# A graph network kernel: index lists loaded a group to a partition and turned on chip, weight fusion moved into the first pass

## The reference, cut to what matters

```python
# layer 0
msg = relu(x[src] + edge_attr)
agg = segment_sum(msg, dst)
h = 2 * x + agg
f = gelu(bn1(h) @ W1.T + b1) @ W2.T + b2
x = layernorm(x + bn2(h + f))
# layer 1
m = gelu((x[src] + edge_attr) @ W1m + b1m) @ W2m + b2m
agg = segment_sum(m, dst) / max(degree, 1)
u = gelu(agg @ W1u + b1u) @ W2u + b2u
x = layernorm(x + layer_norm(x + u) * gamma + beta)
```

## Time and profile before

| | |
|---|---|
| median of 3 runs | 2294.37 us (2292.27 to 2295.15) |
| the profiled execution's own time | 2303.09 us |
| its span | 2301.3 us |
| PE busy | 1904.6 us (83%) |
| POOL busy | 1674.7 us (73%) |
| DVE busy | 1469.5 us (64%) |
| ACT busy | 1115.6 us (48%) |
| DMA packets | 375187, 567.87 MB; 74454 of them under 512 B |

### The profile page before, as it was taken

How to read it: one execution, slowest core, us unless ns; L and a number is a source line. 1 busy time by engine, 2 the same in 40 slices (tenths; PEclk the granted TensorE clock), 3 DMA queues, 4 the chain that set the end, 5 groups by cost and what they waited for, 6 DMA issues and landing times.

```text
span 2301.3 us, 36392 instructions
## 1 busy us (share of the span) xinstructions
PE 1904.6 (83%) x9184; PEld 1564.5 (68%) x9184; DVE 1469.5 (64%) x3241; ACT 1115.6 (48%) x2268; POOL 1674.7 (73%) x1673
## 2 busy tenths in 40 slices
PE   2887887888887887878856998989989898898896
PEld 1776666666666766666745777877777777777774
DVE  2555555555555555555546677777777777777774
ACT  3444434434444444434325555655565565565662
POOL 4777777777777777777637777777777777777770
PEclk9999999999999999999979999999999999999996
DMA  9999898888999999999856777777777777777771
GB/s 181 317 303 294 283 289 284 294 291 289 291 299 288 297 294 287 289 295 289 254 152 201 218 219 227 226 217 229 224 223 230 221 219 224 216 232 220 220 208 37
DMA packets 375187, 567.87 MB, mean 247 GB/s; under 512 B 74454, under 2 KB 241618, under 8 KB 375122
## 3 DMA queue, kind: packets, MB, share of 16 engines
q1 hardware_dynamic: 280060, 347.71, 47.9%
q0 software_dynamic: 79872, 218.21, 31.9%
q10 hardware_dynamic: 15190, 1.28, 0.7%
HBM read 500.51 MB, written 66.49 MB: 246 GB/s over the span
## 4 chain that ended last, share of the span: by engine, by line
POOL 47%; DMA 17%; issue 16%; PE 13%; DVE 5%; ACT 1%; DVEq 0%; ACTq 0%; POOLq 0%
POOL m_all L413 47%; DMA m_all<-in_x,src_p 8%; DMA m_all<-y_scratch,src_u 7%; PE bank L738 5%; PE bank L763 2%; DMA node<-in_dst 2%; DVE bank L1042 1%; PE bank L654 1%; DVE m_all L1031 1%; ACT m_all L538 1%; PE bank L692 1%; PE bank L710 1%; PE bank L796 1%; PE bank L720 1%; DVE m_lo L1047 1%
## 5 line engine op out<-in xcount | busy, mean ns | idle before, releaser
L413 POOL DMA_INDIRECT m_all<-in_x,src_p x832 | 862.8, 1037 | 278.7 <-issue 239.0
L413 POOL DMA_INDIRECT m_all<-y_scratch,src_u x832 | 810.9, 975 | 292.9 <-issue 231.5
L738 PE MATMUL bank<-m_all,sel 128*128 128x257 f32 x1664 | 460.4, 402 | 184.1 <-ACT m_all L538 182.9
L796 PE MATMUL bank<-w1m_sb,e_all 128*128 128x256 f32 x2080 | 535.1, 397 | 92.5 <-DVE m_lo L1047 87.2
L538 ACT ACTIVATE m_all<-m_all 128x512 f32<-128x512 f32 x416 | 261.6, 632 | 579.2 <-DVE m_all L1031 577.0
L1031 DVE TENSOR_TENSOR m_all<-m_all,e_all 128x512 f32<-128x512 f32 x416 | 286.9, 693 | 357.3 <-DMA m_all<-in_x,src_p 355.7
L738 PEld LDWEIGHTS bank<-m_all,sel 128*128 128x128 f32 x1664 | 306.0, 194 | 304.1 <-ACT m_all L538 241.0
L796 PEld LDWEIGHTS bank<-w1m_sb,e_all 128*128 128x128 f32 x2080 | 382.5, 195 | 162.1 <-DVE m_lo L1047 77.0
L1042 DVE TENSOR_TENSOR bank<-bank,m_all 128x512 f32<-128x512 f32 x416 | 290.5, 698 | 258.7 <-DMA m_all<-y_scratch,src_u 233.3
L563 ACT ACTIVATE m_hi<-bank 128x512 fp32r<-128x512 f32 x416 | 248.8, 598 | 405.4 <-DVE bank L1042 400.9
L763 PE MATMUL bank<-w1m_sb,ez 128*128 128x256 f32 x1248 | 331.1, 389 | 6.5 <-issue 6.3
(11 more groups left out here) (133 smaller groups left out, 1852.0 us busy)
## 6 DMA issues: line engine op xcount, KB each, us to landing
e_all<-in_edge SPq DMA_DIRECT2D x416, 256.0 KB, 5.7
e_all<-in_edgeT SPq DMA_DIRECT2D x208, 256.0 KB, 4.1
ez<-in_edgeT SPq DMA_DIRECT2D x104, 384.0 KB, 6.6
z_scratch<-zc SPq DMA_DIRECT2D x104, 384.0 KB, 5.5
e_all<-z_scratch SPq DMA_DIRECT2D x104, 256.0 KB, 3.6
m_all<-in_x,src_p POOLq DMA_INDIRECT x832, 5.4
e_all<-in_edgeT SPq DMA_DIRECT2D x104, 128.0 KB
e_all<-z_scratch SPq DMA_DIRECT2D x104, 128.0 KB
```

The costliest lines, as they stand in the source:

```text
L413: pool.indirect_dma_start(out=m_sb[n % ROUND][:, t, :], out_offset=None, in_=table, in_offset=bass.IndirectOffsetOnAxis(ap=sources[:, g, 2 ...
L738: return pe.matmul(psum[:, 0:D + 1], selection[:, u, :].bitcast(F32), m_all[:, slot, u % 2, 0:D + 1], start=(u == 0), stop=(u == TILES - 1 ...
L796: last = pe.matmul(z_bank(s)[:, t * D:(t + 1) * D], eT_sb[s % ERING][:, k, t * P:(t + 1) * P], w1m_sb[:, k, :], start=(k == 0), stop=(k == ...
```

## The change

- The lists are loaded once each, with a group on each partition: ends_f[i] is [104, 1024], from two transfers, 103 rows of 4096 bytes and the last group's row, both on ACT's queue, dst first. The window starts win_i are loaded as before.
- DVE casts a list, subtracts from dst each row's own first entry (win_col), takes the extent by partition, and masks the repeated edges of the last group. PE turns the lists by 32 transposes of [104, 128], 8 for each of rel_p, src_p, rel_u, src_u, with a step of 8 columns for the first order; DVE copies them out of PSUM. The four lists are [128, 8, G] now.
- POOL takes the sources of the first two groups from a tile of their own, src_0, and waits for lists_made 2 (rel_p and src_p copied) before the third group.
- On SP's queue w1m and ez move in between the edge loads, the weights of the fusion go before the others, and src_p's loads are gone.
- The weight fusion, the bias row and the spreading of b2u move from the setup into steps 6 and 9 of PE's first round; ACT's copies go to steps 8 and 11 of its round, DVE's to step 13. PE enters the first pass at lists_made 4.
- The spreading of the window starts is left to the general path.

```diff
@@ tiles
-        src_p, src_u = sb("src_p", [P, G, TILES], I32), sb("src_u", [P, G, TILES], I32)
-        rel_p, rel_u = sb("rel_p", [P, G, TILES]), sb("rel_u", [P, G, TILES])
+        src_p, src_u = sb("src_p", [P, TILES, G], I32), sb("src_u", [P, TILES, G], I32)
+        rel_p, rel_u = sb("rel_p", [P, TILES, G]), sb("rel_u", [P, TILES, G])
+        src_0 = sb("src_0", [P, 2, TILES], I32)
...
+        ends_f = [flat[0:G, i * GROUP:(i + 1) * GROUP] for i in range(2)]
@@ SP
-            sp.dma_start(src_p[:, 0:2, :], ends(src, 0, 2)).then_inc(src_first, 16)
+            sp.dma_start(src_0[:], src[0:2 * GROUP].rearrange("(g p u) -> p g u", p=P, u=TILES)).then_inc(src_first, 16)
...
-            sp.dma_start(src_p[:, 2:full, :], ends(src, 2, full)).then_inc(src_rest, 16)
-            sp.dma_start(src_p[:, full, :], last_ends(src)).then_inc(src_rest, 16)
...
-                        sp.wait_ge(lists_made, 2)
+                        sp.wait_ge(lists_turned, 4)
@@ POOL
             for n in range(2 * PAIRS):
-                gather(x, src_p, n)
-            pool.wait_ge(src_rest, 32)
+                gather(x, lambda g, u: src_0[:, g, u:u + 1], n)
+            pool.wait_ge(lists_made, 2)
             for n in range(2 * PAIRS, M):
                 if n >= ROUND:
                     pool.wait_ge(pair_summed, n - ROUND + 1)
-                gather(x, src_p, n)
+                gather(x, lambda g, u: src_p[:, u, g:g + 1], n)
@@ ACT
-            act.dma_start(dst_i[:, full, :], last_ends(dst)).then_inc(dst_in, 16)
-            act.dma_start(dst_i[:, 0:full, :], ends(dst, 0, full)).then_inc(dst_in, 16)
-            for array, tile in ((src, ends_i[0]), (dst, ends_i[1])):
-                act.dma_start(tile[:, 0:blocks * P].rearrange("t (b p) -> t b p", p=P),
-                              array[0:blocks * P * P].rearrange("(b t p) -> t b p", t=P, p=P)).then_inc(lists_in, 16)
...
+            for i, array in enumerate((dst, src)):
+                act.dma_start(ends_i[i][0:full, :], array[0:full * GROUP].rearrange("(g e) -> g e", e=GROUP)
+                              ).then_inc(ends_in[i], 16)
+                act.dma_start(ends_i[i][full:G, :], array[E - GROUP:E].rearrange("(a e) -> a e", a=1)
+                              ).then_inc(ends_in[i], 16)
...
+                if known(i) and i == 0:
+                    if s == 8:
+                        keep_weights()
+                    if s == 11:
+                        keep_bias()
@@ PE
+            def turn_ends(i, by_place, to):
+                rows = ends_f[i].rearrange("g (p u) -> g u p" if by_place else "g (u p) -> g u p", u=TILES)
+                for u in range(TILES):
+                    last = pe.transpose(bank[to + u // 4][:, u % 4 * G:(u % 4 + 1) * G], rows[:, u, :], ident[0:G, 0:G])
+                last.then_inc(lists_turned, 1)
...
+            pe.wait_ge(ends_ready, 1)
+            turn_ends(0, True, 0)
+            pe.wait_ge(extent_ready, 1)
+            pe.matmul(bank[7][:, 0:1], ones[:], extent[:, 2:3], start=True, stop=True).then_inc(counted, 1)
+            pe.wait_ge(ends_ready, 2)
+            turn_ends(1, True, 2)
+            turn_ends(0, False, 4)
+            pe.wait_ge(general_made, 1)
+            turn_ends(1, False, 6)
+            pe.wait_ge(lists_made, 4)
+            pe.wait_ge(w1m_in, 16)
...
+            def fuse_weights():
+                pe.wait_ge(consts_in, 16 * 7)
...
+                if known(i) and i == 0:
+                    if s == 6:
+                        fuse_weights()
+                    if s == 9:
+                        fuse_bias()
@@ DVE
+            dve.wait_ge(ends_in[0], 32)
+            link(dve.tensor_copy(ends_f[0], ends_i[0]))
+            link(dve.tensor_copy(win_col[0:G, :], ends_f[0][:, 0:1]))
+            link(dve.tensor_scalar(ends_f[0], ends_f[0], win_col[0:G, :], None, ALU.subtract))
+            dve.tensor_reduce(extent[0:G, 0:1], ends_f[0], AX_X, ALU.min)
+            link(dve.tensor_reduce(extent[0:G, 1:2], ends_f[0], AX_X, ALU.max))
...
+            dve.wait_ge(ends_in[1], 32)
+            dve.tensor_copy(ends_f[1], ends_i[1]).then_inc(ends_ready, 1)
             dve.wait_ge(counted, 1)
+            dve.tensor_scalar(general[:], bank[7][:, 0:1], 1.0, None, ALU.min).then_inc(general_made, 1)
+            for i, to in enumerate((rel_p, src_p, rel_u, src_u)):
                 dve.wait_ge(lists_turned, i + 1)
+                for half in range(2):
+                    last = dve.tensor_copy(to[:, 4 * half:4 * half + 4, :],
+                                           bank[2 * i + half][:, 0:4 * G].rearrange("p (u g) -> p u g", g=G))
+                last.then_inc(lists_made, 1)
...
-                positions = rel[:, g, :] if known(g) else rel[:, bass.ds(g, 1), :].rearrange("p a u -> p (a u)")
-                select(q % 2, positions.unsqueeze(2)).then_inc(sel_made, 1)
+                select(q % 2, rel[:, :, g:g + 1] if known(g) else rel[:, :, bass.ds(g, 1)]).then_inc(sel_made, 1)
```

More of the change, by code:

```diff
@@ L84, in build @@
     TURN = 512 - (KD + 1) * WIN
-    assert M == ROUND * C and G > full and KH == 2 * KD and G <= 512 and CHUNK % 2 == 0 and N % 2 == 0
+    assert M == ROUND * C and G > full and KH == 2 * KD and G <= P and CHUNK % 2 == 0 and N % 2 == 0
     chunks = [(c * CHUNK, min(CHUNK, N - c * CHUNK)) for c in range(C)]
@@ L467, in _, with keep_weights, keep_bias @@
             is_general = act.value_load(general[0:1, 0:1], min_val=0, max_val=1)
+            def keep_weights():
+                act.wait_ge(w_fused, 1)
+                for k in range(KD):
+                    act.copy(wmu_sb[:, k, :], bank[2 + k][:]).then_inc(w_kept, 1)
+            def keep_bias():
+                act.wait_ge(w_fused, 2)
+                act.copy(bmu_hi[:], bank[2][0:1, :]).then_inc(w_kept, 1)
             def node_a(i, s):
@@ L622, in _ @@
         def _(pe):
-            pe.wait_ge(win_ready, 1)
-            pe.matmul(bank[7][:, 0:G], ones[0:1, :], win_f[:], start=True, stop=True).then_inc(win_spread, 1)
-            pe.wait_ge(extent_ready, 1)
-            pe.matmul(bank[6][:, 0:1], ones[:], extent[:, 2:3], start=True, stop=True).then_inc(counted, 1)
-            pe.wait_ge(consts_made, 5)
-            for i in range(2):
-                pe.wait_ge(lists_float, i + 1)
-                for b in range(TB):
-                    tiles = min(P, T - b * P)
-                    last = pe.transpose(bank[2 + 2 * i + b // 4][:, b % 4 * P:b % 4 * P + tiles],
-                                        ends_f[i][0:tiles, b * P:(b + 1) * P], ident[0:tiles, 0:tiles])
-                last.then_inc(lists_turned, 1)
@@ L635, in _ @@
-            pe.wait_ge(consts_in, 16 * 8)
-            pe.wait_ge(vt_in, 16)
-            pe.wait_ge(general_made, 1)
-            for i in range(KD):
-                for k in range(KD):
-                    pe.matmul(bank[i][:], w2mT_sb[:, k, i * P:(i + 1) * P], w1u_sb[:, k, :],
-                              start=(k == 0), stop=(k == KD - 1))
-            for k in range(KD):
-                last = pe.matmul(bank[6][0:1, :], vec("b2m", k), w1u_sb[:, k, :], start=(k == 0), stop=(k == KD - 1))
@@ new lines, in _, with fuse_bias @@
+            is_general = pe.value_load(general[0:1, 0:1], min_val=0, max_val=1)
+            def fuse_weights():
+                pe.wait_ge(consts_in, 16 * 7)
+                for i in range(KD):
+                    for k in range(KD):
+                        last = pe.matmul(bank[2 + i][:], w2mT_sb[:, k, i * P:(i + 1) * P], w1u_sb[:, k, :],
+                                         start=(k == 0), stop=(k == KD - 1))
+                last.then_inc(w_fused, 1)
+            def fuse_bias():
+                pe.wait_ge(vt_in, 16)
+                pe.wait_ge(w_kept, KD)
+                for k in range(KD):
+                    pe.matmul(bank[2][0:1, :], vec("b2m", k), w1u_sb[:, k, :], start=(k == 0), stop=(k == KD - 1))
+                pe.matmul(bank[3][:, 0:D], ones[0:1, :], b2u_row[:].rearrange("a k p -> a (k p)"), start=True, stop=True
+                          ).then_inc(w_fused, 1)
@@ L859, in _ @@
             with pe.If(is_general > 0):
+                pe.wait_ge(win_ready, 1)
+                pe.matmul(bank[0][:, 0:G], ones[0:1, :], win_f[:], start=True, stop=True).then_inc(win_spread, 1)
+                fuse_weights()
+                fuse_bias()
                 groups(pe, sums_general, 1, C)
@@ L1218, in first_pass @@
                     selection(rel_p, 0, *after)
+                if known(i) and i == 0 and s == 13:
+                    keep_rest()
                 node_a(i, s)
```

121 lines of the change are left out of this document (42 added, 79 removed).

## The result

| | before | changed |
|---|---|---|
| median of 4 runs, us | 2294.24 (2292.27 to 2295.15) | 2308.64 (2305.29 to 2311.77) |
| profiled execution, us | 2303.09 | 2307.26 |
| span of that execution, us | 2301.3 | 2305.5 |

The changed kernel takes 1.0064 times as long (95% interval 1.0046 to 1.0081): 14.4 us slower, where 11 were forecast.

What follows compares the result with a forecast made beforehand. POOL's gathers were taken to set the pace; POOL going on later, +13.4 us, less the ring wait that goes, 2.45, gave +11 us: 2305 us for the median, range 2295 to 2318, with chance 0.62.

Steps and rivals of the forecast that it cites:

- What bounds it: First pass: POOL's nearly back-to-back gathers set the pace, 1.348 us apart; only 16.5 us of gaps wait for the tensor engine.
- One engine for 103 rows: List loads: a transfer counting 103 on the outside goes through one of the 16 DMA engines, as 103 is prime.
- The landing: Setup: the source list lands at 54 us, sharing one engine with SP's packets and the gathers.
- the bound of 60: Source list's landing: 60 us if all of SP's packets come before the lists on the shared engine.
- From the landing to POOL: Setup: cast, 8 transposes, two copies and semaphores take 4.2 us; POOL goes on at 58.4 instead of 44.96, +13.4 us.
- The wait that goes: Start of first pass: POOL's 2.75 us wait for the first ring slot drops to 0.30, -2.45 us.
- The moved fusion, free: Steps 6 and 9 of the first pass: the moved products cost nothing under the tensor engine's lead; uncovered, 8.6 us.
- Strided selection, free: DVE's selections from positions 416 bytes apart: taken as costing nothing; +8 us if their time doubled.
- The clearing of acc near 4 us: Setup on ACT: the 16.02 us copy that clears acc begins at about 4 us, not 37.93; worth nothing by itself.
- Rival A: List loads spread over all engines, so POOL's hole goes: mid -22 us, 2272 us; chance 0.18.
- Rival B: ACT's queue served first on the one engine: landing at 47, +4 us, 2298 us, or sooner and no difference; chance 0.12.
- Rival C: The first pass's start, not POOL, sets its end: +3 us, or -36 with the lists spread; chance 0.08.

Runs made afterwards that it cites:

- the second job: Follow-up runs in which the kernel before took 2297.88 us; it held the cuts at 96 and 94, 96 with fusion in setup, and 103 rows first on SP.
- 96 rows: Changed kernel with each list's 103 rows loaded as two transfers of 96 and 7 rows: 2279.49 us, 0.9923 of the kernel before.
- 96 rows, fusion in setup: Changed kernel with lists cut into 96 and 7 rows and the weight fusion put back into the setup: 2284.43 us, 0.9928 of the kernel before.
- 94 rows: Changed kernel with each list's 103 rows loaded as transfers of 94 and 9 rows: 2290.89 us, 0.9971 of the kernel before.
- 103 rows, first on SP: Changed kernel with both uncut lists moved from ACT's queue to SP's, ahead of the edge rows: 2300.87 us, 1.0014 of the kernel before.
- the first job: Follow-up runs in which the kernel before took 2698.06 us; lists cut at 96 gave 0.9945 of it, at 94 rows 1.0005.
- the three doses: List transfers of 103, 94 and 96 rows in the changed kernel; source list there at 58.14, 36.62 and 15.35 us or sooner.
- the first and third jobs: Follow-up runs in which the kernel before took 2698.06 and 2680.07 us; the third reran the changed kernel (1.007) and the cut at 96 (0.9909).

## Why the prediction was right

The start of gather 33 orders all runs of the comparison and of the second job. Its shift against the kernel before, as a part of 2294 to 2298 us, beside the ratio; the last gather of the pass, number 832, shows whether the pass ends by as much earlier or later:

| kernel | first product, shift | gather 33, us | shift | gather 832, shift | gather 33 as a ratio | measured |
|---|---|---|---|---|---|---|
| 96 rows | -34.4 | 44.69 | -23.1 | -26.9 | 0.990 | 0.9923 (0.9903 to 0.9943) |
| 96 rows, fusion in setup | -17.4 | 50.35 | -17.4 | -15.6 | 0.992 | 0.9928 (0.9905 to 0.9952) |
| 94 rows | -15.2 | 61.39 | -6.4 | -10.5 | 0.997 | 0.9971 (0.9954 to 0.9988) |
| 103 rows, first on SP | -7.2 | 69.28 | +1.5 | -0.8 | 1.001 | 1.0014 (0.9998 to 1.0029) |
| changed | +5.8 | 82.41 | +14.7 | +9.4 | 1.006 | 1.0064 (1.0046 to 1.0081) |

By the ratios all but the first agree within 0.1%. By the medians the first has won 18.4 us of its 23.1 and the second 13.5 of its 17.4; what takes the rest wasn't followed up. The shift is still there 800 gathers later, lower by 2 to 5 us in four of the five, which points at the one profile that all are measured against. The runs of the first job are not in the table for the reason given there: with 94 rows gather 33 came at 59.69, 8 us before 67.75, and no time was won. The first product orders them too, but its size is off by 0.4 to 0.7% in four of the five, and the fourth has the wrong sign. Point by point:

- **What bounds it.** Held in the comparison and the second job. Behind the first gather, POOL's gaps in the first pass are 0.30 us of issue and the waits at gathers 17 and 33, and nothing longer. The 16.5 us that the earlier trace rows put down to the tensor engine are 46 gaps, and only the 2.75 us among them is a wait. It did not hold in the slower jobs.
- **One engine for 103 rows.** Shown by the three doses, and by the 6.8% and 26 GB/s of the queues.
- **The landing.** The term that was mis-sized: 54 us forecast, 58.14 measured, within the bounds of 47 and 60. The failed step is the share of SP's packets, taken as 147 to 206 from the earlier trace rows, where most of ACT's packets are 32-byte pieces. The last constant of SP's queue was issued until 58.46, so nearly all that SP had came before the end of the list, which is the case of the bound of 60. The rate given to the one engine, 25.6 GB/s, held (26).
- **From the landing to POOL.** 4.2 us forecast, 61.93 - 58.14 = 3.8 measured. The eight transposes of every eighth column at 40.66 take 1.63 us, 0.20 each, less than the 0.256 of the sum; the 24 at 58.89, eight of which are of this kind, take 4.42. The plain ones behind the 0.256 turn 128 columns and not 104, so whether the step costs something isn't shown; twice the price is excluded. POOL went on 16.97 us later, not 13.4, for the landing's 4 us less the 0.4 gained here.
- **The wait that goes.** 2.45 forecast, 16.97 - 14.66 = 2.3 measured. The first product came at 69.48 and not at 66.6, by the late landing. That the wait is back at 2.86 with 103 rows and the fusion in the setup shows that it goes only because the fusion moved as well.
- **The moved fusion, free.** Held. Its products stand at 82.49 and 91.20 us, and every gather around them has its 0.30 us of issue and no more. The eight big ones took 3.60 us, not the 6.05 of the setup.

```profile
82.49 3.60 PE L646 MATMUL bank<-node 128*128 128x512 f32 x8
...
83.75 0.95 POOL L406 DMA_INDIRECT m_all<-in_x,src_p  x1 [0.30 <-issue]
...
91.20 1.88 PE L654 MATMUL bank<-node,vt_sb 128*1 128x512 f32 x4
```

- **Strided selection, free.** Held. The group of that line among DVE's in the changed kernel has a mean of 820 ns, the 0.82 us of the earlier trace rows:

```profile
L991 DVE TENSOR_TENSOR sel<-iota,rel_p 128x640 fp32r<-128x640 f32 x104 | 85.2, 820 | 16.1 <-PE bank L747 12.0 <-issue 4.1
```

- **The clearing of acc near 4 us.** Wrong: it began at 41.71, because ACT's queue hung on the one-row issues until 40.4. It cost nothing, since it was done at 57.73 and the first product came at 69.48. With 96 rows it begins at 6.04.
- **Rival A** did not come true but was sized well: it gave -22 us for spread lists; cut to spread, they gave -18.4 by the medians. Rival B fell with the landing at 58.14. Rival C fell as a bound of the whole, and is true in part, as the second gate.

The 11 us forecast and the 14.4 measured differ by the landing, and nothing else of size cancels out in the sum: +16.97 and -2.3 for +13.4 and -2.45.

Left open: what in the first and third jobs held every kernel, the one before among them; where the first two rows of the table lose their 4 to 5 us; and whether a list padded to 112 rows does better than 96 and 7, which wasn't tried.

## What to carry to other kernels

Look at the outer count of every large load before its size: 103 rows of 4 KB came at the speed of one DMA engine, and cut into 96 and 7 both lists were there before 15.4 us and not at 58.1. When POOL, or whatever sets the pace, has more than one gate ahead of it, find the latest one and move that; opening the other (the source list sent first in the kernel before) gained nothing, and what it pushed back cost 3 us by the traces. Setup work moved under the cover of the main loop pays only by what the gate behind it was late: by POOL's starts 2.6 us here with slow lists, 5.7 with quick ones.

## What was not expected

A transfer of one row (4 KB) behind one of 103 rows on the same queue takes 11.38 and 25.71 us to issue; behind 96 and 7 rows it takes 0.27 and 0.54. On SP's queue it is 20.18 us for the second list's single row, in the run that puts the lists there. So a slow transfer also stops the queue's engine, and all that this engine was to do next, which is how acc's clearing came to wait 36 us. The loads of the other queue came later as well: SP's last constant was being issued until 58.46 us in the changed kernel and until 30.02 with 96 rows.
